# A selective-scan phase: preparation passes through PSUM, one product moved from GpSimd to VectorE, a seventh readout moved to GpSimd

## The reference, cut to what matters

```
u  = silu(conv(in_proj(seq)));  z = in_proj(seq)
dt = softplus(dt_proj(x_proj(u)) + dt_proj_b);  Bm, Cm = x_proj(u)
for each token t:  h = exp(dt*A) * h + (dt*u) * Bm
                   y = sum over the 16 states of h * Cm
out = out_proj((y + u*D) * silu(z))
```

## Time and profile before

| | |
|---|---|
| median of 3 runs | 2171.5 us |
| the profiled execution | 2169.19 us |
| its span in the profile | 2167.4 us |
| busy: PE, VectorE (DVE), ScalarE (ACT), GpSimd (POOL) | 1599.9, 1304.6, 1031.5, 1156.8 us |
| granted TensorE clock, mean | 0.875 of full speed |

### The profile page before, as it was taken

How to read it: one execution, slowest core, us unless ns; L and a number is a source line. 1 busy time by engine, 2 the same in 40 slices (tenths; PEclk the granted TensorE clock), 3 DMA queues, 4 the chain that set the end, 5 groups by cost and what they waited for, 6 DMA issues and landing times. The chain is left out here.

```text
span 2167.4 us, 26308 instructions
## 1 busy us (share of the span) xinstructions
PE 1599.9 (74%) x4872; PEld 834.2 (38%) x4873; DVE 1304.6 (60%) x2262; ACT 1031.5 (48%) x1696; POOL 1156.8 (53%) x1151
## 2 busy tenths in 40 slices
PE   4477777777777379999971367777777778289993
PEld 3122222223246146666640122222223327256662
DVE  4399999999986001111117289999999996211102
ACT  5567776776752022322321466677776772121111
POOL 2399899998851700000017189989998891400004
PEclk9799999998985689999985689999999995589995
DMA  6677777777745342111113487777777772223313
GB/s 215 149 174 170 169 171 172 168 171 167 170 93 190 90 129 75 46 44 45 47 48 105 123 187 165 170 169 171 168 170 168 168 170 70 72 73 111 110 64 95
DMA packets 104909, 283.47 MB, mean 131 GB/s; under 512 B 19789, under 2 KB 78429, under 8 KB 94013
## 3 DMA queue, kind: packets, MB, share of 16 engines
q1 hardware_dynamic: 96680, 265.34, 50.3%
q0 software_dynamic: 8192, 17.71, 2.8%
HBM read 225.80 MB, written 57.18 MB: 131 GB/s over the span
## 5 line engine op out<-in xcount | busy, mean ns | idle before, releaser
L699 POOL TENSOR_TENSOR mamba_dbu<-mamba_rep 128x462 f32<-128x462 f32 x640 | 680.3, 1087 | 45.4 <-DMA mamba_rep<-dt_rows 44.5
L558 PE MATMUL mamba_ysum<-mamba_hc,all_sel 128*128 128x462 f32 x800 | 446.7, 645 | 243.3 <-DVE mamba_hc L753 242.2
L646 ACT ACTIVATE mamba_state<-mamba_rep,all_m_acol 128x462 f32<-128x462 f32 x640 | 390.0, 640 | 267.3 <-DVE mamba_last L768 266.3
L771 DVE TENSOR_TENSOR_SCAN mamba_state<-mamba_state,mamba_carry,mamba_dbu 128x462 f32<-128x462 f32 x400 | 453.8, 1171 | 7.7 <-ACT mamba_state L646 7.7
L558 PEld LDWEIGHTS mamba_ysum<-mamba_hc,all_sel 128*128 128x128 f32 x800 | 135.4, 203 | 527.7 <-DVE mamba_hc L753 507.4
L768 DVE TENSOR_TENSOR_SCAN mamba_last<-mamba_state,mamba_last,mamba_dbu 128x462 f32<-128x462 f32 x240 | 280.0, 1166 | 35.4 <-ACT mamba_state L646 23.0
L694 POOL TENSOR_TENSOR mamba_hcp<-mamba_last,mamba_rep 128x462 f32<-128x462 f32 x240 | 266.2, 1109 | 9.4 <-DVE mamba_last L768 8.1
L1225 DVE TENSOR_TENSOR experts_h<-experts_sg,experts_up 128x512 f32<-128x512 f32 x62 | 42.6, 688 | 371.5 <-PE experts_up L1120 313.8
L753 DVE TENSOR_TENSOR mamba_hc<-mamba_state,mamba_rep 128x462 f32<-128x462 f32 x400 | 248.1, 623 | 0.0
L553 PE MATMUL mamba_ysum<-mamba_hcp,all_sel 128*128 128x462 f32 x480 | 247.4, 599 | 0.0
L290 POOL MEMSET seq_mhalf<- 96x3 f32 x2 | 0.2, 98 | 362.0 <-POOLq L1460 362.0
(11 more groups left out here) (173 smaller groups left out, 2262.6 us busy)
## 6 DMA issues: line engine op xcount, KB each, us to landing
mamba_rep<-bc_rows SPq DMA_DIRECT2D x168, 462.0 KB, 6.9
mamba_rep<-dt_rows SPq DMA_DIRECT2D x168, 462.0 KB, 7.4
dt_rows<-mamba_dd SPq DMA_DIRECT2D x168, 115.5 KB, 7.0
weights_w<-in_L_w_dram SPq DMA_DIRECT2D x16, 1024.0 KB, 9.7
mamba_xs<-seq_scratch SPq DMA_DIRECT2D x92, 116.0 KB, 9.3
experts_xs<-slot_rows SPq DMA_DIRECT2D x62, 128.0 KB
expert_rows<-experts_eo SPq DMA_DIRECT2D x62, 128.0 KB, 1.7
slot_rows<-setup_zero SPq DMA_DIRECT2D x11, 512.0 KB
```

The source lines that it names most:

```text
L558: nc.tensor.matmul(ysum[:, 0:TC], sel[:, i // NM, :], hc[:, n % HCD, :], start=False, stop=end).then_inc(hc_summed, 1)
L646: nc.scalar.activation(state[:, STATE_BANK[i], 0:TC], rep[:, par * REP_ROWS + i // NM, :], ACT.Exp, scale=m["acol"][:, i:i + 1]).then_inc( ...
L699: pool.tensor_tensor(dbu[:, i % 4, :], rep[:, first + NG + i // NM, :], rep[:, first + 2 * NG + i % NM, :], ALU.mult).then_inc(dbu_ready, 1)
L771: nc.vector.tensor_tensor_scan(bank, bank, dbu[:, i % 4, :], carry[:, i:i + 1], ALU.mult, ALU.add).then_inc(scan_done, 1)
```

## The change

ON_POOL becomes (0, 2, 5, 7, 10, 12, 14): GpSimd reads out seven items and VectorE nine, with pairs (3,4) and (8,9) and five single items. SUM_ORDER becomes 1, 0, 3, 4, 2, 6, 5, 8, 9, 7, 11, 10, 13, 12, 14, 15. ScalarE writes 1+ex and Ln into the two PSUM banks of `front` in place of SBUF tiles, so each of VectorE's three passes has one PSUM operand; TensorE's next use of `front` waits for VectorE in place of ScalarE. VectorE makes dt*u itself, behind dt. The pass `rr` is issued behind item 14, the others behind the last readout. AT_ONE goes from 11 to 10, AT_BC from 13 to 12, AT_LN from 15 to 13. SyncE stores the dt rows as the first thing in a chunk.

```diff
-ON_POOL = (0, 3, 6, 8, 11, 13)
+ON_POOL = (0, 2, 5, 7, 10, 12, 14)
...
-AT_SILU, AT_EXP, AT_ONE, AT_LN, AT_BC, AT_DT, AT_DTU = 6, 10, 11, 15, 13, 5, 2
+AT_SILU, AT_EXP, AT_ONE, AT_LN, AT_BC, AT_DT, AT_RR = 6, 10, 10, 13, 12, 5, 14
...
             def store_dt(k):
-                sp.wait_ge(front_pool, START + k + 1)
+                sp.wait_ge(front_dve, START + DVES * k + D_DTU)
...
+                store_dt(k + 1)
                 sp.wait_ge(decay_ready, items_before)
                 sp.wait_ge(dbu_ready, items_before)
                 sp.wait_ge(hc_ready, START + ND * k)
                 sp.wait_ge(hcp_ready, START + NP_ * k)
                 sp.wait_ge(rep_loaded, replicas_before)
                 replicate_bc(k + 1)
-                store_dt(k + 1)
                 replicate_dt(k + 1)
...
             def prep_u(k):
                 pe.wait_ge(xs_loaded, 32 * (k + 1))
-                pe.wait_ge(front_act, START + ACTS * k)
+                pe.wait_ge(front_dve, START + DVES * k)
...
             def prep_one(k):
                 act.wait_ge(front_act, START + ACTS * k + A_EXP)
-                nc.scalar.activation(w1[:, :], ex[:, :], ACT.Copy, bias=1.0).then_inc(front_act, 1)
+                nc.scalar.activation(front[:, 0, 0:TC], ex[:, :], ACT.Copy, bias=1.0).then_inc(front_act, 1)
 
             def prep_ln(k):
-                nc.scalar.activation(ln[:, :], ex[:, :], ACT.Ln, bias=1.0).then_inc(front_act, 1)
+                act.wait_ge(front_act, START + ACTS * k + A_BC)
+                nc.scalar.activation(front[:, 1, 0:TC], ex[:, :], ACT.Ln, bias=1.0).then_inc(front_act, 1)
...
-                pool.tensor_tensor(dd[:, 1, :], dd[:, 0, :], u_k, ALU.mult).then_inc(front_pool, 1)
...
-                        if i == AT_DTU:
-                            prep(k + 1)
...
+            def prep_rr(k):
+                dve.wait_ge(front_act, START + ACTS * k + A_ONE)
+                nc.vector.scalar_tensor_tensor(out=rr[:, :], in0=front[:, 0, 0:TC], scalar=1.0, in1=ex[:, :],
+                                               op0=ALU.subtract, op1=ALU.subtract).then_inc(front_dve, 1)
+
+            def prep_dt(k):
                 done = START + DVES * k
                 dve.wait_ge(front_act, START + ACTS * k + A_LN)
                 dve.wait_ge(front_dve, done + D_R)
-                nc.vector.tensor_tensor(lr[:, :], ln[:, :], rr[:, :], ALU.subtract).then_inc(front_dve, 1)
+                nc.vector.tensor_tensor(front[:, 1, 0:TC], front[:, 1, 0:TC], rr[:, :], ALU.subtract).then_inc(front_dve, 1)
...
-                nc.vector.tensor_tensor(dd[:, 0, :], lr[:, :], rx[:, :], ALU.add).then_inc(front_dve, 1)
+                nc.vector.tensor_tensor(dd[:, 0, :], front[:, 1, 0:TC], rx[:, :], ALU.add).then_inc(front_dve, 1)
+                dve.wait_ge(front_dve, done + D_DT)
+                nc.vector.tensor_tensor(dd[:, 1, :], dd[:, 0, :], chunk_of(dve, u, k), ALU.mult).then_inc(front_dve, 1)
...
                         if i - 1 in ON_DVE:
                             read_out(i - 1)
+                        if i == AT_RR:
+                            prep_rr(k + 2)
                     read_out(ITEMS - 1)
-                    prep(k + 2)
+                    prep_dt(k + 2)
```

More of the change, by code:

```diff
@@ L397, in phase_mamba @@
         u, sz = sb("u", [P, UBUFS, TC]), sb("sz", [P, UBUFS, TC])
-        ab, ex, w1, ln, rx = sb("ab", [P, TC]), sb("ex", [P, TC]), sb("w1", [P, TC]), sb("ln", [P, TC]), sb("rx", [P, TC])
-        rr, lr = sb("rr", [P, TC]), sb("lr", [P, TC])
+        ab, ex, rx, rr = sb("ab", [P, TC]), sb("ex", [P, TC]), sb("rx", [P, TC]), sb("rr", [P, TC])
         dd = sb("dd", [P, 2, TC])
@@ L415, in phase_mamba @@
         xs_loaded, rep_loaded, bc_stored, dt_stored = sem("xs_loaded"), sem("rep_loaded"), sem("bc_stored"), sem("dt_stored")
-        front_mm, front_act, front_dve, front_pool = sem("front_mm"), sem("front_act"), sem("front_dve"), sem("front_pool")
+        front_mm, front_act, front_dve = sem("front_mm"), sem("front_act"), sem("front_dve")
         decay_ready, dbu_ready, scan_done, carry_done = sem("decay_ready"), sem("dbu_ready"), sem("scan_done"), sem("carry_done")
@@ L424, in phase_mamba @@
         A_U, A_Z, A_ABS, A_RELU, A_EXP, A_ONE, A_BC, A_LN, ACTS = 1, 2, 3, 4, 5, 6, 7, 8, 8
-        D_R, D_LR, D_DT, DVES = 1, 2, 3, 3
+        D_R, D_LR, D_DT, D_DTU, DVES = 1, 2, 3, 4, 4
         REPS = 2 * NS
@@ L563, in _ @@
                         prep_bc(k + 2)
-            pe.wait_ge(front_act, START + ACTS * (NCH + 2))
+            pe.wait_ge(front_dve, START + DVES * (NCH + 2))
             for t in range(NT):
@@ L667, in _ @@
         def _(pool):
-            for s in (dbu_ready, front_pool, hcp_ready):
+            for s in (dbu_ready, hcp_ready):
                 pool.sem_inc(s, START)
[L670 to L679, removed]
-                pool.tensor_tensor(dd[:, 1, :], dd[:, 0, :], u_k, ALU.mult).then_inc(front_pool, 1)
-            prep(0)
             with pool.Fori(0, NCH // 2) as pair:
@@ L718, in _ @@
                 dve.sem_inc(s, START)
-            def prep(k):
+            def prep_rr(k):
[3 more added lines that the diff above has]
+            def prep_dt(k):
                 done = START + DVES * k
-                dve.wait_ge(front_act, START + ACTS * k + A_ONE)
-                nc.vector.scalar_tensor_tensor(out=rr[:, :], in0=w1[:, :], scalar=1.0, in1=ex[:, :],
-                                               op0=ALU.subtract, op1=ALU.subtract).then_inc(front_dve, 1)
                 dve.wait_ge(front_act, START + ACTS * k + A_LN)
                 dve.wait_ge(front_dve, done + D_R)
-                nc.vector.tensor_tensor(lr[:, :], ln[:, :], rr[:, :], ALU.subtract).then_inc(front_dve, 1)
+                nc.vector.tensor_tensor(front[:, 1, 0:TC], front[:, 1, 0:TC], rr[:, :], ALU.subtract).then_inc(front_dve, 1)
                 if not (isinstance(k, int) and k == 0):
@@ L731, in prep @@
                 dve.wait_ge(front_dve, done + D_LR)
-                nc.vector.tensor_tensor(dd[:, 0, :], lr[:, :], rx[:, :], ALU.add).then_inc(front_dve, 1)
+                nc.vector.tensor_tensor(dd[:, 0, :], front[:, 1, 0:TC], rx[:, :], ALU.add).then_inc(front_dve, 1)
+                dve.wait_ge(front_dve, done + D_DT)
+                nc.vector.tensor_tensor(dd[:, 1, :], dd[:, 0, :], chunk_of(dve, u, k), ALU.mult).then_inc(front_dve, 1)
             for k in range(2):
-                prep(k)
+                prep_rr(k)
+                prep_dt(k)
             with dve.Fori(0, B) as b:
```

## The result

The changed kernel takes 2260.2 us (median of 4 runs, 2259.07 to 2261.39) against 2171.4 for the kernel before in the same comparison: a ratio of 1.0411, 95% interval 1.0393 to 1.0429. It is 89 us slower; 68 were forecast, and the range, 2192 to 2270, holds it. The profiled execution took 2261.39 us, with a span of 2259.8.

What follows compares the result with a forecast made beforehand. VectorE was taken to set the pace at 26.77 us a chunk; 25.98 + 0.25 + 2.2 + 0.1 = 28.5, +1.75 times 40, less about 1 us in each of two layers, is +68 on 2171.5: 2239 us, range 2192 to 2270.

Steps and rivals of the forecast that it cites:

- step 5: ScalarE's serial chain between items 10 and 14: VectorE stalls 0.6 us before scan 11 and 1.6 before scan 14, each chunk.
- the 2.3 of the sum: Per chunk, the stalls from ScalarE's chain, 2.2 us, together with 0.1 for ScalarE's writes into PSUM.
- The extra 0.1: ScalarE writing 1+ex and Ln into PSUM instead of SBUF: between 0 and 0.2 us more a chunk, taken as 0.1.
- steps 1 to 4: VectorE's own work per chunk: -0.54, +0.05, -0.73, +0.62, -0.19, from 26.77 to 25.98 us, or 26.23 with dt*u's wait.
- the +0.25: dt*u on VectorE waiting behind GpSimd's third product: +0.25 us a chunk, with 0 and 1.07 as ends.
- The collision that was named as a rival: dt*u on VectorE stands behind a whole GpSimd product each time: +0.8 us more a chunk, 2271 us; chance 0.12.
- step 6: SyncE storing the dt rows first, ahead of the B and C replicas: cost nothing, with about 1 us cover to GpSimd.
- ScalarE keeping up: Rival: decay 14 is ready when scan 13 ends, so only VectorE's own work counts: 2148 us; chance 0.10.
- only the least stall: Rival: decay 11 is on time and only 1.2 us of stall stays a chunk: 2196 us; chance 0.12.
- replicas late: Rival: DMA work ends 6 us later, the next chunk waits a microsecond or more: 2280 us and up; chance 0.02.
- one-PSUM passes don't relieve `rr`: Rival: VectorE passes with one SBUF input wait for GpSimd too, so rr stays at 1.3 us: 2268 us; chance 0.04.
- 5.5 us into 4.3: ScalarE's work from the end of item 10's scan to scan 14: 5.5 us must fit in 4.3, at least 1.2 stall.

Runs made afterwards that it cites:

- experiment 1: The changed kernel with AT_LN put back from 13 to 15, nothing else: 2175.7 us, ratio 1.0033 to the kernel before.
- experiment 2: The changed kernel with AT_LN put back from 13 to 15 and AT_ONE from 10 to 11: 2152.2 us, ratio 0.9923 to the kernel before.
- experiment 3: The changed kernel with item 12 summed by TensorE ahead of item 13 instead of behind it: 2234.4 us, ratio 1.0297 to the kernel before.
- experiment 7: The kernel of experiment 2 with SyncE's store of the dt rows back behind the B and C replication: 2143.8 us, ratio 0.9877 to the kernel before.
- experiment 8: The kernel of experiment 2 with the kernel before's six GpSimd items in place of seven: 2187.8 us, ratio 1.0087 to the kernel before.
- experiment 4: The kernel before with only 1+ex and Ln into PSUM and TensorE's next use of front waiting for VectorE: 2167.2 us, ratio 0.9988.
- experiment 9: The kernel before with the PSUM operands, the change's seven GpSimd items and item 12 summed ahead of 13; dt*u stays on GpSimd: 2118.1 us, ratio 0.9757.

## Why the prediction was right, and what it lacked

- *The chain on ScalarE (step 5)* was right in place, mechanism and nearly in size: 1.55 us measured for 1.6 before scan 14, 0.47 for 0.6 before scan 11. Experiments 1 and 2 show that both stalls go with the two numbers AT_LN and AT_ONE alone. What the two cost is more than the 2.02 us shown: a chunk takes 28.45 us with them (experiment 3) and 26.21 without (experiment 7), 2.24 for the 2.3 of the sum (the two kernels differ in SUM_ORDER and in SyncE's store as well). The extra 0.1 for ScalarE's writes into PSUM was not there: 1+ex takes 0.56 us into PSUM and 0.58 into SBUF, Ln 0.56 and 0.59.
- *VectorE's own work (steps 1 to 4)*: 26.21 us a chunk in experiment 7, where dt*u stands behind GpSimd in 4 of 44 passes, against 25.98 without its wait and 26.23 with it. `rr` is at 0.63, and the stall before item 7 went. *dt\*u* was right in sum only: the +0.25 was meant as a wait behind GpSimd. In the changed kernel its duration never exceeds 0.643 us, and it is 0.20 us late for another reason, its dependence on dt and a register step ahead of it. Nor is GpSimd out of its way there, as GpSimd's timeline of the changed kernel shows (the product under way when dt*u starts, then all four):

```profile
323.33 1.16 POOL L686 TENSOR_TENSOR mamba_dbu<-mamba_rep 128x462 f32<-128x462 f32 x1
```
```profile
321.25 4.65 POOL L686 TENSOR_TENSOR mamba_dbu<-mamba_rep 128x462 f32<-128x462 f32 x4
```

  dt*u starts at 324.40, 0.1 us before the product from 323.33 ends; it goes on time, and GpSimd's next product is the one that waits (1.16 us in the median of all, 1.45 at most). The collision that was named as a rival appeared in experiments 1, 2 and 8, where dt*u often comes in the middle of a product. The missing stall before scan 14 is not the reason, as experiment 7 has no such stall and hardly a collision. What goes with it is GpSimd's waiting for replicas: 29, 36 and 32 times in experiments 1, 2 and 8, 2 in the changed kernel, 4 in experiment 7.
- *The step that failed* is the sum's silence on y: nothing was entered for PE's last sums. The last chunk of a layer of the kernel before shows the margin already: `rr` takes 0.63 us there, as GpSimd has nothing left to do, and y waits. From VectorE's timeline of the kernel before:

```profile
630.96 0.64 DVE L780 TENSOR_TENSOR mamba_y<-mamba_ysum,mamba_sz 128x462 f32 x1 [0.54 <-PE mamba_ysum L558]
```

  That row was to be had before the prediction and was not priced. In the changed kernel it holds at the higher clock and fails at the lower: 1.06 us in 23 of 40 chunks, 24.4 us, which is more than the 21 us between 2239 and 2260. The other terms were 3 to 4 us too high together. That the range holds the result owes something to its width, as no case that it was made from was this one.
- *SyncE's order (step 6)* was entered at nothing. In the changed kernel GpSimd waits for replicas only at the start of a phase and dt*u never stands behind it, so nothing shows there; no run put the order back in that kernel. In the kernel without the stalls it costs 8 us, most likely by way of GpSimd's products and dt*u.
- *Rivals.* ScalarE keeping up, only the least stall, and replicas late fell with the profile. That one-PSUM passes don't relieve `rr` fell too.
- *The fixed costs*: `rr` takes 0.64 us with one PSUM input in experiment 4 and `lr` 0.65, against 0.632 and, for dt, 0.640 at best with both in SBUF. The Trainium skill's figures (VectorE: DVE Perf Modes, section on the trn2 errata: 58 cycles from SBUF, 120 from PSUM) would make the difference 0.065 us, an estimate; the trace shows under 0.01 for either pass.
- *VectorE and GpSimd in each other's way*: `rr` takes 1.219 us in the median with both inputs in SBUF beside a busy GpSimd and 0.639 with one in PSUM, and when dt*u comes first it is GpSimd's product behind it that takes up to 1.45 us in place of 1.16. The Trainium skill, SBUF — State Buffer, section "SBUF: two separate sides", states it as an exclusive lock on a shared pair of ports between GpSimd and a VectorE instruction with two SBUF inputs, held by whichever starts first; the trace agrees.

## What to carry to other kernels

A serial engine with idle time in the mean can still set the pace: count what it must do between the event that frees a resource and the moment its result is wanted (5.5 us into 4.3 by the prediction's count), table loads included, before a step is moved into that window. Where two engines end a stretch at nearly the same time, an edit to either shows almost nothing alone (2.5 and 2 us), while the pair is worth far more than the two together (33 us); a wait that a rare case of the trace before shows, as the last chunk's, gives the margin. When a change of several parts loses, undo its schedule numbers first: here two of them hid a gain of 0.8%.

## What the runs showed that I had not expected

- A stall upstream can cost twice, through TensorE's clock. In chunks with the stall before scan 14 PE rested 2.60 us ahead of its last sums, and in 23 of 40 it then ran some of them at the lower of its two levels (1.2 GHz; 3.18 us for four matmuls instead of 1.71). With the rest at 1.84 us (experiment 3) or the stall gone (1) no tail runs at the lower level and no y waits. In three chunks the lower level cost something earlier too: PE was at it from 1394.2 to 1401.0 us, for one, the Abs behind its dt projection started only at 1402.61, and the stall before item 11 was 1.08 us in place of 0.47. Why the clock fell in one chunk and not in the next, with the same 2.60 us ahead, stays open; it wasn't tried.
- The idle time that the profile shows before an instruction is less than what the wait costs. y's wait of 0.54 us (experiment 4), once gone, gave 0.72 a chunk (26.78 to 26.06). Instructions that follow each other without a wait overlap: with the wait, dt to y to the next scan takes 1.17 and 0.96 us from start to start, without it 0.56 and 0.88 (experiment 9).
